# Mamba blocks with shared experts on one Trainium2 core: out projection with standing weights, ten pair additions, and the pre-work's places on TensorE and ScalarE

## What is computed

```python
xz = x @ Wi.T;  xs, z = split(xz)              # 256 inner channels
u  = silu(conv4(xs) + cb);  dt, B, C = split(u @ Wx.T)
dt = softplus(dt @ Wdt.T + bdt);  A = -exp(Alog)   # 16 states
h  = exp(dt*A) * h + dt * B * u;  y = sum_s h * C  # scan over 128 tokens
y  = (y + u * Dp) * silu(z);  x = x + y @ Wo.T
```

## Time and profile before

| | us |
|---|---|
| median of 3 runs | 2886.13 (2884.73 to 2886.28) |
| the profiled execution | 2885.38 |
| its span, first to last instruction | 2883.6 |

### The profile page before, as it was taken

One profiled execution on the slowest core, in us unless ns is written; L12 is line 12 of the kernel. 1 busy time (PEld: TensorE's weight loads), 2 busy tenths in 40 slices (PEclk: granted clock), 3 DMA queues, 4 the chain that ended last, 5 costly groups with the idle time before them and its releaser, 6 DMA issues. The chain is left out here.

```text
span 2883.6 us, 23236 instructions
## 1 busy us (share of the span) xinstructions
PE 2454.6 (85%) x6258; PEld 1087.5 (38%) x6258; DVE 2060.6 (71%) x2022; ACT 1547.3 (54%) x2398; POOL 2007.4 (70%) x1234
## 2 busy tenths in 40 slices
PE   5488898998998888888888888988888699999586
PEld 3133333433333333333333333333333244444364
DVE  4389999999999887777777787787778633333221
ACT  2367767767766655565556565555665233232132
POOL 3389999999997877777777777777777622222176
PEclk9799998998899989999999999999999799999798
DMA  7345645644646666555555655666555330000154
GB/s 207 142 144 188 231 158 170 226 165 139 203 157 220 213 210 217 181 187 186 185 198 200 202 176 206 206 213 209 187 185 176 130 104 15 31 15 9 38 113 72
DMA packets 217995, 462.39 MB, mean 160 GB/s; under 512 B 29644, under 2 KB 111506, under 8 KB 217746
## 3 DMA queue, kind: packets, MB, share of 16 engines
q1 hardware_dynamic: 204178, 449.66, 46.9%
q0 software_dynamic: 11264, 7.98, 1.8%
q10 hardware_dynamic: 2432, 3.38, 0.3%
HBM read 437.51 MB, written 23.99 MB: 160 GB/s over the span
## 5 line engine op out<-in xcount | busy, mean ns | idle before, releaser
L811 DVE TENSOR_TENSOR_SCAN hh<-dA,psdB 128x1024 f32<-128x1024 f32 x512 | 1168.0, 2285 | 79.8 <-ACT dA L717 19.9
L886 POOL TENSOR_TENSOR gg<-hh,Clo 128x1024 f32<-128x1024 f32 x408 | 960.5, 2356 | 373.3 <-DVE hh L811 368.1
L554 PE MATMUL psY<-gg,ident 128*128 128x512 f32 x1776 | 922.7, 648 | 82.3 <-POOL gg L890 43.7
L717 ACT ACTIVATE dA<-dt,Acur 128x508 f32<-128x508 f32 x1024 | 668.1, 708 | 21.3 <-DVE hh L811 20.4
L800 DVE TENSOR_TENSOR psdB<-psT,Blo 128x1024 f32<-128x1024 f32 x395 | 483.2, 1223 | 112.5 <-ACT psT L692 99.5
L554 PEld LDWEIGHTS psY<-gg,ident 128*128 128x128 f32 x1776 | 341.0, 202 | 581.7 <-issue 381.2
L1276 DVE TENSOR_TENSOR ac<-sg,d_bank 128x512 f32<-128x512 f32 x144 | 99.1, 688 | 242.9 <-PE d_bank L1126 189.9
L730 ACT ACTIVATE late<-psdB 128x512 f32<-128x512 f32 x144 | 86.0, 597 | 312.2 <-PE psdB L580 312.2
L535 PE MATMUL psW<-xnT,wcur 128*128 128x512 f32 x512 | 234.7, 600 | 20.6 <-DMA diag<-diags_l 18.8
L886 POOL TENSOR_TENSOR gg<-hh,late 128x1024 f32<-128x1024 f32 x104 | 243.7, 2359 | 12.1 <-PE psY L554 8.4
L1175 ACT ACTIVATE sg<-d_bank 128x512 f32<-128x512 f32 x144 | 86.0, 597 | 261.0 <-PE d_bank L1122 255.0
(11 more groups left out here) (168 smaller groups left out, 2953.1 us busy)
## 6 DMA issues: line engine op xcount, KB each, us to landing
Blo<-rows SPq DMA_DIRECT2D x280, 512.0 KB, 5.3
Clo<-rows SPq DMA_DIRECT2D x280, 512.0 KB, 4.8
late<-rows SPq DMA_DIRECT2D x104, 512.0 KB, 6.4
wcur<-taps_l SPq DMA_DIRECT2D x32, 512.0 KB
disp<-fw SPq DMA_DIRECT2D x16, 528.0 KB, 8.1
dx<-disp SPq DMA_DIRECT2D x16, 528.0 KB
fw<-in_Wg SPq DMA_DIRECT2D x32, 256.0 KB, 5.0
fw<-in_Wu SPq DMA_DIRECT2D x32, 256.0 KB, 4.6
```

Of the source, the lines that this page charges most:

```text
L554: ins = pe.matmul(psY[:, :], lhsT=ident[:, :], rhs=gg[k % NGB][:, j, :], start=False, stop=(k % NK == NK - 1 and j == last - 1))
L717: ins = act.activation(dA[k % NDA][:, j, :, 1:T], dt[i % 2][:, c, :, 1:T], ACT.Exp, scale=Acur[i % 2][:, s:s + 1])
L811: dve.tensor_tensor_scan(out=hh[k % NHB][:, :, :].rearrange("p c t -> p (c t)"), data0=dA[k % NDA][:, :, :, :].rearrange("p c q t -> p (c ...
L886: ins = pool.tensor_tensor(gg[k % NGB][:, :, :], hh[k % NHB][:, :, :], tile(Clo, Chi, slot(i, s)), ALU.mult)
```

## The change

- Out projection: `project` ("outT", TensorE step 8) multiplies with wo as the stationary operand, two 512-column matmuls, giving the transposed delta in psW. ScalarE copies it to yg's first half (`place_delta`, step 13). `turn_back` ("out", TensorE step 9) adds residents (identity, 512 columns) and the delta by four 128-column matmuls with yg as the stationary operand and the identity as the moving one. psW gets one more use per iteration.
- PAIRED gets steps 7 and 9, so ten in place of eight.
- AHEAD says for which iteration a piece of pre-work is. x0 is made in step 14 for i + 2 (before: in step 0 for i + 1). x1 goes from step 1 to 0, z0 and z1 from 2 to 1 and 2, bcdt from 5 to 4, dt0 and dt1 from 6 to 6 and 7, out from 8 to 9, the transposes from 13 to 12.
- On ScalarE the pieces go one or so step sooner, silu from 8 to 7 and sums0 ahead of the softplus; sums1 goes from 3 to 4 and stands ahead of x0's copy.
- In step 8 TensorE does skip and sum behind the dense matmuls and the work of PE_AT; in step 0 that was so before.
- New places of gate, up, down and product (V_AT and C_AT now have lists of their own), of transpose_x and place_sum; weights(i + 2) is issued in step 10.

```diff
-PE_AT = {0: ["x0"], 1: ["x1"], 2: ["z0", "z1"], 5: ["bcdt"], 6: ["dt0", "dt1"], 8: ["out"], 13: ["transposes"]}
-ACT_AT = {1: ["params", "dtu1"], 2: ["turn0", "norm"], 3: ["sums1"], 5: ["x0"], 6: ["x1"], 7: ["z0", "z1"], 8: ["silu"], 10: ["turn1", "bcdt"], 11: ["dt0", "dt1"],
-          12: ["softplus", "sums0"], 13: ["centre"], 14: ["added"], 15: ["dtu0"]}
+AHEAD = {"x0": 2, "x1": 1, "z0": 1, "z1": 1, "bcdt": 1, "dt0": 1, "dt1": 1, "outT": -1, "out": -1, "T": 2}
+PE_AT = {0: ["x1"], 1: ["z0"], 2: ["z1"], 4: ["bcdt"], 6: ["dt0"], 7: ["dt1"], 8: ["outT"], 9: ["out"], 12: ["T"], 14: ["x0"]}
+SUM_FIRST = (1, 2, 3, 4, 5, 6, 7, 9, 10, 11, 12, 13, 14, 15)
+ACT_AT = {1: ["params", "dtu1", "norm"], 2: ["turn0"], 4: ["sums1", "x0"], 5: ["x1"], 6: ["z0"], 7: ["z1", "silu"], 10: ["bcdt", "turn1"], 11: ["dt0"],
+          12: ["sums0", "dt1", "softplus"], 13: ["outT"], 14: ["added"], 15: ["centre", "dtu0"]}
...
-G_AT = [-9, -8, -6, -5, -4, -3, -2, -1, 3]
-U_AT = [6, 8, 9, 11, 12, 14, 15, 19, 20]
-D_AT = [10, 10, 11, 13, 14, 18, 18, 21, 22]
-T_AT = 5
-PAIRED = [0, 1, 2, 5, 8, 13, 14, 15]
+G_AT = [-8, -7, -6, -5, -4, -3, -2, 0, 1]
+C_AT = [-3, -2, -1, 0, 1, 2, 3, 5, 6]
+U_AT = [5, 7, 9, 10, 12, 13, 15, 17, 19]
+V_AT = [7, 9, 10, 12, 13, 15, 17, 19, 21]
+D_AT = [9, 9, 10, 12, 13, 15, 17, 19, 21]
+T_AT = 4
+P_SUM = 11
+PAIRED = [0, 1, 2, 5, 7, 8, 9, 13, 14, 15]
...
-                        if k == 11 and i + 2 < NIT:
+                        if k == 10 and i + 2 < NIT:
                             weights(i + 2)
...
-                def out_projection(t):
+                def project(t):
                     pe.wait_ge(ygated, NH * (t + 1))
+                    pe.wait_ge(wfree, W["outT", t])
+                    for c in range(NH):
+                        ins = pe.matmul(psW[:, :], lhsT=wo[:, layer(t) * NH + c, :], rhs=yg[t % 2][:, c, :], start=(c == 0), stop=(c == NH - 1))
+                    ins.then_inc(wready, 1)
+
+                def turn_back(t):
                     pe.wait_ge(wfree, W["out", t])
                     pe.matmul(psW[:, :], lhsT=ident[:, :], rhs=flat(group(t)), start=True, stop=False)
                     for q in range(G):
-                        for c in range(NH):
-                            ins = pe.matmul(psW[:, q * T:(q + 1) * T], lhsT=yg[t % 2][:, c, q * T:(q + 1) * T], rhs=wo[:, layer(t) * NH + c, :], start=False, stop=(q == G - 1 and c == NH - 1))
+                        ins = pe.matmul(psW[:, q * T:(q + 1) * T], lhsT=yg[t % 2][:, 0, q * T:(q + 1) * T], rhs=ident[:, :], start=False, stop=(q == G - 1))
                     ins.then_inc(wready, 1)
...
                 transposes(1)
+                pre(1, "x0")
                 for i in range(NIT):
                     for k in range(NSTEP):
-                        if k == NK:
-                            skip(i, 1)
-                        if k > 0:
+                        if k in SUM_FIRST:
                             sum_states(i, k)
...
+                        work(i, k)
+                        if k % NK == 0:
+                            skip(i, k // NK)
+                        if k not in SUM_FIRST:
                             sum_states(i, k)
...
+                def place_delta(t):
+                    act.wait_ge(wready, W["outT", t] + 1)
+                    act.activation(yg[t % 2][:, 0, :], psW[:, :], ACT.Copy).then_inc(wfree, 1)
...
-                        for n in stream([a + 2 for a in U_AT], i, k):
+                        for n in stream(V_AT, i, k):
                             act_product(n)
```

More of the change, by code:

```diff
@@ L269, in psw_uses @@
 def psw_uses():
-    order = [("T", 0)] + [(what, 0) for k in sorted(PE_AT) for what in PE_AT[k] if what in PRE] + [("T", 1)]
+    order = [("T", 0)] + [(what, 0) for what in PRE] + [("T", 1), ("x0", 1)]
     for i in range(NIT):
@@ L274, in psw_uses @@
             for what in PE_AT[k]:
[L275 to L281, removed]
+                t = i + AHEAD[what]
+                if 0 <= t < NIT:
+                    order.append((what, t))
+    order += [("outT", NIT - 1), ("out", NIT - 1)]
     return {use: n for n, use in enumerate(order)}
@@ L595, in down, with work @@
                     pe.matmul(psD[:, :], lhsT=fwd[:, e % NXW, f, :], rhs=sg[:, n % NSLG, :], start=(n % NST == 0), stop=(n % NST == NST - 1)).then_inc(downed, 1)
+                def work(i, k):
+                    for what in PE_AT.get(k, ()):
+                        t = i + AHEAD[what]
+                        if not 0 <= t < NIT:
+                            continue
+                        if what in PRE:
+                            pre(t, what)
+                        if what == "outT":
+                            project(t)
+                        if what == "out":
+                            turn_back(t)
+                        if what == "T":
+                            transposes(t)
                 transposes(0)
[L598 to L601, removed]
+                for what in PRE:
+                    pre(0, what)
                 transposes(1)
+                pre(1, "x0")
                 for i in range(NIT):
                     for k in range(NSTEP):
-                        if k == NK:
-                            skip(i, 1)
-                        if k > 0:
+                        if k in SUM_FIRST:
                             sum_states(i, k)
@@ L616, in _ @@
                             gate(n)
[L617 to L625, removed]
+                        work(i, k)
+                        if k % NK == 0:
+                            skip(i, k // NK)
+                        if k not in SUM_FIRST:
                             sum_states(i, k)
-                out_projection(NIT - 1)
+                project(NIT - 1)
+                turn_back(NIT - 1)
             @block.scalar
@@ L744, in _ @@
                 centre(0)
-                for k in sorted(ACT_AT):
-                    for what in ACT_AT[k]:
-                        pre(0, what)
+                for what in ("params", "norm", "x0", "x1", "z0", "z1", "silu", "bcdt", "dt0", "dt1", "softplus"):
+                    pre(0, what)
                 centre(1)
@@ L753, in _ @@
                             move_given(i, k - 1)
-                        for n in stream([a + 5 for a in G_AT], i, k):
+                        for n in stream(C_AT, i, k):
                             place_gate(n)
@@ L757, in _ @@
                             place_x((i - FIRST + 1) // NF)
[L758 removed]
+                        if k == P_SUM and i > FIRST and (i - FIRST) % NF == 0:
                             place_sum((i - FIRST) // NF - 1)
@@ L764, in _ @@
                                 centre(i + 2)
+                            if what == "outT" and i > 0:
+                                place_delta(i - 1)
                             if what == "added" and i > 0:
@@ L781, in _ @@
                 copy_sums(NIT - 1, 1)
+                place_delta(NIT - 1)
                 added(NIT - 1)
```

## The result

The changed kernel is slower: 2916.61 us (2915.41 to 2917.74, 4 runs) against 2886.2 us, ratio 1.0104 with a 95% interval of 1.0087 to 1.0122. The forecast was 2817 us. The profiled execution's span is 2915.4 us, 31.8 more than before.

A forecast was written before the change was run, and what follows sets the result against it. In later iterations no engine is full; VectorE's product wait, set by late TensorE, decides. 64.2 + 0.7 + 2.1 + 3.3 + 2.9 + 0.8 = 74.0 us per iteration, about -69 us in all: 2817 us (own range 2798 to 2840; overall 2775 to 2868).

The forecast's parts named there:

- the frame of the sum: Iterations of the 16-to-28 kind: 64.2 us without VectorE's product and psT waits, plus the remaining stands, gives 73.2 us.
- Skip, dt and z waits, psT: Skip's 3.20 us go; dt and z waits fall mostly behind sums; exponentials and psT lose 2.1 in place of 3.8 us.
- The one-step products: Products 2 and 4, now one step behind their ups: VectorE stands 3.3 and 2.9 us per iteration.
- Product 7: Product behind x0 and x1 in steps 14 and 0: VectorE stands 0.7 us.
- The clock term: TensorE stands between steps 5 and 7: one stretch at the half clock is kept, worth 0.8 us per iteration.
- B: Rival: low clock over steps 7 to 9 makes one-step products cost 2.4 us more net; 2853 us, chance 0.18.
- C: Rival: TensorE falls behind at the boundary, low clock in steps 14 to 1; slower, 2930 us, chance 0.12.
- The pair additions: Steps 7 and 9: GpSimd +2 x 1.27 us, TensorE -2 x 0.86; each addition makes its sum 1.27 us later.
- Silu ends 0.3 us ahead of need: ScalarE in iterations 1 to 12: silu costs 0, bounds -0.6 and +1.2 us each.
- Out projection: On TensorE, from 2.65 to 3.47 us, 0.8 us more per iteration; the ScalarE copy is made in time.
- Start, end: Iteration 0 loses 3 us to exponentials behind x0; project, place_delta and turn back add 1.6 us at the very end.
- iteration 30: Iteration near the end, counted in the sum as 3 us saved.

The follow-up runs named there:

- the run both: Changed kernel with products 2 and 4 (and their downs) one VectorE step later and silu behind the decay of step 7; 2768.3 us, 0.9596.
- both_eight: Changed kernel with products 2 and 4 one VectorE step later, silu behind step 7's decay, and eight pair additions instead of ten; 2740.6 us, 0.9499.
- best_eight: Changed kernel with products 2 and 4 a step later, silu behind step 7's decay, eight pair additions and the old out projection; 2747.3 us, 0.9522.
- two_steps: Changed kernel with products 2 and 4 (and their downs) one VectorE step later, so every product lies two steps behind its up; 2803.3 us, 0.9718.

## Why the prediction was wrong, point by point

For iterations 16 to 29 the frame of the sum was right: VectorE's iteration without its stands is 64.6 us (64.2 forecast), and 64.6 + 12.9 before products + 0.9 before psT and scan 7 are the 78.4 measured. The term that failed is the product stands with the clock behind them: 6.9 + 0.8 us forecast, 12.9 measured. That and its like in iterations 15 and 30 make most of the 100 us between forecast and result; 22 are the silu block's, in iterations 1 to 12, for which I had 0.

- *Skip, dt and z waits, psT.* The skip's and most of the dt waits went, psT and scan 7 stand 0.6 + 0.3 us per iteration (I had 2.1). The wait for z0's copy, which I had expected to fall mostly behind a sum, went up instead, from 0.9 to 1.5 us (20.8 us in 14 iterations).
- *The one-step products.* The chain sums were right: 3.3 and 2.9 us forecast, 3.6 and 3.1 in the iterations where the clock was high and GpSimd had no L922 in between. In the mean they are 5.5 and 3.7. Product 7 was forecast 0.7 and measured 0.7. Products 6 and 8, for which I had nothing, stand 2.3 and 0.7.
- *The clock term is the step that failed in the later iterations.* "One stretch at the half clock, worth 0.8 us" should have been about 10 us of low clock per iteration, worth 3.5 us by the zero matmuls (78.4 to 74.9). I had named B (low clock over steps 7 to 9) and C (low clock in steps 14 to 1) as two rivals with 0.18 and 0.12; the trace has both, each behind a stand that the change makes itself: the addition of step 7 and product 4. How much low clock there is was not what changed: the trace of the kernel before has 12.4 us of it per iteration, in two stretches, of which I had read one (6.9 us), and after has 10.1. What changed is where it lies: within 5 us of an iteration's start the kernel before has none at any of the 14 starts from 17 to 30, after has some at 13. I took C's condition as not met because the change lays no new wait in front of step 14, although I had the 2.9 us stand of product 4, which is that wait, passed on through scan 14 and GpSimd. 73.2 + 0.8 was forecast; with the clock held high, and 5.1 us more matmuls, the run gave 74.9, without them 78.4.
- *The pair additions.* Counted as 1.7 us of TensorE gained and GpSimd's 2.5 hidden. The load was no bound. The two cost 23 us in the changed kernel. In the kernel of the run both, where they were taken out one by one, the addition of step 7 costs 22 us, that of step 9 2 us, which is within the spread of the runs, the two 28. I had written that an addition makes its sum 1.27 us later, but put that price only into product 2's chain, for step 9; the addition of step 7 stood in no term.
- *Iterations 1 to 12.* "Silu ends 0.3 us ahead of need", with bounds of -0.6 and +1.2 us. Measured: scan 7 stands 0.8 to 3.7 us there, 2.75 in the mean; the iterations grew by 1.8 us each, 22 us in all, and with silu one step later they take 54.8, under the 55.2 of before. That the block's place is the cause is shown by the silu run. Why my walk put it too early was not tested; I had gone from x0 to z1 without TensorE's place in iterations in which sum 15, x1 and the skip follow each other.
- *Out projection.* +0.8 us of TensorE was right as a price: with start-to-start times of 429 ns for a 512-column record and 112 ns for a 128-column one, both_eight spends 3.5 us on it and best_eight 2.6. It was not a fixed time: 15 us in the changed kernel, all of it from iteration 15 on, 6.5 in both, less than nothing with eight additions. The Trainium skill's gaps ("TensorE: Matmul & The Clock Gate", Back-to-back issue gap) would make it a small gain of TensorE time; the traces don't agree, by the times just given. That both_eight is 6.7 us faster than best_eight in spite of this price lies, as I read it, in where the stands fall (product 3's above); it was not tested.
- *Start, end.* Start +3 forecast, -0.1 measured; the end +1.6 forecast, 4.7 measured from iteration 31 on; iteration 30 -3 forecast, +8.6 measured. Iteration 30 is the same ring: products stand 17.4 us in it instead of 6.4 (product 2 8.4, product 4 5.8), psT's wait gave back 4.2 and scan 7's took 1.5. In two_steps it takes 72.7 us, where after has 82.7. What makes the end longer than forecast stays open.

Not settled: why the clock falls behind the stand before sum 7 in eight of the 14 iterations and not in the six others, also of the same layer (2.12 us of stand in iteration 16, 2.12 in 17); what decides that was not tried. That product 2 stands 3.6 us or up to 7.6 follows from it.

## What to carry to other kernels

Where one engine's work releases another's through a third, write down for each consumer the chain from the event that it must follow, and keep that distance: two list entries one step too tight cost 113 us here. A stand of TensorE may be paid twice: look at which matmuls come right behind it, since here they ran at the low clock in eight iterations of 14. And TensorE, 86% busy in iterations 16 to 29 of after, was not relieved by taking two sums' matmuls from it, since that made it wait (the run both is 28 us slower than both_eight).

## What the runs showed of the hardware that I had not expected

Six matmuls of zeros per iteration, 5.1 us more work for the engine on which the others wait, made the changed kernel 57 us faster (2916.6 to 2859.5), with the granted clock up from 0.94 to 1.00. Added to a schedule whose stands were mostly gone, the same six changed 5 us. Where TensorE stood anyway, a filler that changes nothing paid; the better way was to remove the stand (both_eight, clock 0.99, 2740.6 us, 5.0% under the kernel before).
